# Three, two and two chunks to a batch, groups of experts chosen by sorting, and a new pace table for the GpSimd queue, in a fused sequence-mixer and mixture-of-experts kernel

## What is computed

```python
y = rmsnorm(x); y_conv = conv3(y); y_ssm = scan(h -> tanh(a) * h + b * y)
x = x + y_conv + y_ssm
x1 = layernorm(x_in + x + (silu(z @ w_gate) * (z @ w_up)) @ w_down)      # z = rmsnorm(x)
scores = sigmoid(x1 @ gate_w.T); choice = scores + gate_bias             # 64 experts, 8 groups of 8
group_scores = sum(top_k(choice in groups, 2))                           # best two of each group
mask = groups of top_k(group_scores, 4); top = top_k(where(mask, choice, 0), 8)
w = scores[top] / sum * 2.5
out = layernorm(x1 + sum over top of w * expert(x1) + shared(x1))        # each expert 128 -> 88 -> 128
```

## Time and profile before

| | us |
|---|---|
| median of 3 runs | 884.73 |
| profiled execution | 877.03 |
| its span in the trace | 875.2 |
| TensorE busy | 687.7 (79%) |
| VectorE busy | 481.7 (55%) |
| ScalarE busy | 338.8 (39%) |
| POOL busy (448 indirect DMAs) | 448.5 (51%) |
| chain that ended last: TensorE | 48% |
| same: VectorE | 17% |
| same: "another core or an unknown queue" | 14% |
| same: "issue" | 14% |

### The profile page before, as it was taken

How to read it: one execution, slowest core, us unless ns; L and a number is a source line. 1 busy time by engine, 2 the same in 40 slices (tenths; PEclk the granted TensorE clock), 3 DMA queues, 4 the chain that set the end, 5 groups by cost and what they waited for, 6 DMA issues and landing times.

```text
span 875.2 us, 13683 instructions
## 1 busy us (share of the span) xinstructions
PE 687.7 (79%) x3808; PEld 539.0 (62%) x3809; DVE 481.7 (55%) x1223; ACT 338.8 (39%) x673; POOL 448.5 (51%) x463
## 2 busy tenths in 40 slices
PE   4986777877577689898898889951499899488994
PEld 3654555554344578787788879940488786255662
DVE  3488466872166546555555566710135357275877
ACT  7772544623322134444334444520144443042332
POOL 0002755656656766666676662067466644667300
PEclk9998878998688799999999999985599999799998
DMA  8998931101201246666666666642276646131100
GB/s 272 420 291 341 410 159 40 44 33 45 96 34 40 72 146 188 183 180 186 189 179 184 183 174 189 185 117 64 77 192 184 176 133 205 48 93 45 28 24 24
DMA packets 141798, 128.49 MB, mean 147 GB/s; under 512 B 11542, under 2 KB 127086, under 8 KB 141294
## 3 DMA queue, kind: packets, MB, share of 16 engines
q1 hardware_dynamic: 127430, 98.73, 36.3%
q0 software_dynamic: 14336, 29.39, 10.8%
HBM read 56.77 MB, written 71.30 MB: 146 GB/s over the span
## 4 chain that ended last, share of the span: by engine, by line
PE 48%; DVE 17%; another core or an unknown queue 14%; issue 14%; ACT 5%; DVEq 1%; DMA 0%; ACTq 0%; SPq 0%
PE OT L863 9%; PE GU L843 9%; PE HT L852 4%; PE XT L832 4%; PE GU L900 3%; PE GU L901 3%; PE XT L909 3%; PE OT L645 2%; DVE arena L1483 2%; PE GU L624 2%; PE GU L625 2%; DVE key L1570 1%; ACT x1r L981 1%; PE OT L791 1%
## 5 line engine op out<-in xcount | busy, mean ns | idle before, releaser
L538 POOL DMA_INDIRECT xs_dram<-x1r,slots x224 | 226.9, 1013 | 203.8 <-DVE slots L1357 78.3
L546 POOL DMA_INDIRECT arena<-os_dram,slots x224 | 219.4, 980 | 168.3 <-DMA os_dram<-ol 54.9
L1474 DVE TENSOR_TENSOR mlpw_sb<-GU,mlpw_sb 128x352 f32<-128x352 f32 x104 | 54.5, 524 | 200.5 <-ACT mlpw_sb L1097 111.1
L843 PE MATMUL GU<-wgu_sb,arena 128*128 x832 | 151.6, 327 | 3.5 <-issue 2.9
L863 PE MATMUL OT<-wd_sb,arena 88*128 x832 | 116.2, 283 | 28.5 <-issue 26.4
L843 PEld LDWEIGHTS GU<-wgu_sb,arena 128*128 128x128 f32 x832 | 130.8, 198 | 10.3 <-issue 9.9
L863 PEld LDWEIGHTS OT<-wd_sb,arena 88*128 88x128 f32 x832 | 102.6, 194 | 38.9 <-issue 38.6
L1107 ACT ACTIVATE ol<-OT 128x512 f32<-128x512 f32 x104 | 62.0, 596 | 163.2 <-PE OT L863 97.5
L852 PE MATMUL HT<-ident,mlpw_sb 128*88 128x128 f32 x416 | 63.9, 277 | 33.4 <-DVE arena L1483 31.8
L1090 ACT ACTIVATE arena<-XT 128x512 f32<-128x512 f32 x104 | 61.9, 596 | 46.1 <-remote 26.8
L832 PE MATMUL XT<-ident,arena 128*128 128x128 f32 x416 | 66.7, 284 | 14.1 <-ACT arena L1090 12.8
(11 more groups left out here) (183 smaller groups left out, 913.5 us busy)
## 6 DMA issues: line engine op xcount, KB each, us to landing
arena<-xs_dram SPq DMA_DIRECT2D x104, 256.0 KB
os_dram<-ol SPq DMA_DIRECT2D x104, 256.0 KB
xs_dram<-ol SPq DMA_DIRECT2D x8, 2048.0 KB, 14.6
xs_dram<-ol SPq DMA_DIRECT2D x4, 2560.0 KB
wgu_sb<-wgu_dram SPq DMA_DIRECT2D x1, 5632.0 KB
xs_dram<-x1r,slots POOLq DMA_INDIRECT x224
arena<-os_dram,slots POOLq DMA_INDIRECT x224
wd_sb<-wd_dram SPq DMA_DIRECT2D x1, 2816.0 KB
```

The source lines that it names most:

```text
L538: g.indirect_dma_start(out=xs[b], out_offset=bass.IndirectOffsetOnAxis(ap=slots[:, c:c + 1], axis=0), in_=x1r[:, t, :], in_offset=None).th ...
L546: return g.indirect_dma_start(out=gbuf[:, c % 2, i, k, :], out_offset=None, in_=os[batch_of(c)], in_offset=bass.IndirectOffsetOnAxis(ap=sl ...
L843: ins = mm(GU[:, 2 * r + i // 2, (i % 2) * 2 * I:(i % 2 + 1) * 2 * I], xg[:, r, i * P:(i + 1) * P], wgu_sb[:, bass.ds(at[i], 2 * I)], star ...
```

## The change

Three edits are made together.

Batches: the first batch takes chunks 0, 1 and 2 (40 quads), the second 3 and 4 (32), the third 5 and 6 (32). `EARLY` becomes 2. `Q0` becomes 0, 40, 72, 104. Chunk 1 is summed from quad 68 on instead of 64, and the sums, statistics and one root in the dense stage move by 0 to 2 steps.

Routing: the best two of each group are found by pairwise maxima and minima. The best four groups are found by sorting (`max` gives a row's 8 values in order), the last four of the sorted values are overwritten, and `match_replace` marks the others in the scores.

POOL's table: `POOL_AT`, `FRONT_END`, `SHARED_AT` and `QUADS_AT` get new numbers.

```diff
-BATCHES = (2, 3, 2)
+BATCHES = (3, 2, 2)
...
-SUM_AT = (14, 16, 21, 24)
+SUM_AT = (14, 17, 21, 24)
...
-SUMS_IN_DENSE = {6: 4, 21: 5, 36: 6}
-STATS_IN_DENSE = {0: 0, 1: 1, 2: 2, 3: 3, 14: 4, 29: 5}
+SUMS_IN_DENSE = {8: 4, 22: 5, 36: 6}
+STATS_IN_DENSE = {0: 0, 1: 1, 2: 2, 3: 3, 16: 4, 30: 5}
...
-ROOT_AT = (5, 30)
+ROOT_AT = (5, 31)
...
-POOL_AT = 86.0
+POOL_AT = 100.0
...
-QUADS_AT = 261.0
+QUADS_AT = 256.0
...
+            pairs = flat(group[:, 0:3, :]).rearrange("p (g n) -> p g n", n=3)
...
-                then(v.tensor_reduce(m1, ch4, AX_X, ALU.max))
-                then(v.tensor_tensor(ta4, ch4, bc(m1.unsqueeze(2), P, n, EG), ALU.is_equal))
-                v.tensor_reduce(ties, ta4, AX_X, ALU.add)
-                then(v.scalar_tensor_tensor(out=tb4, in0=ta4, scalar=-BIG, in1=ch4, op0=ALU.mult, op1=ALU.add))
+                lo, hi = ch4[:, :, 0:EG // 2], ch4[:, :, EG // 2:EG]
+                v.tensor_tensor(ta4[:, :, 0:4], lo, hi, ALU.max)
+                then(v.tensor_tensor(ta4[:, :, 4:8], lo, hi, ALU.min))
+                v.tensor_tensor(tb4[:, :, 0:2], ta4[:, :, 0:2], ta4[:, :, 2:4], ALU.max)
+                v.tensor_tensor(tb4[:, :, 2:4], ta4[:, :, 0:2], ta4[:, :, 2:4], ALU.min)
+                then(v.tensor_tensor(tb4[:, :, 4:6], ta4[:, :, 4:6], ta4[:, :, 6:8], ALU.max))
...
-                v.tensor_reduce(m2, tb4, AX_X, ALU.max)
-                then(v.tensor_scalar(ties, ties, 1.5, -BIG, ALU.is_lt, ALU.mult))
-                then(v.tensor_tensor(ties, ties, m1, ALU.add))
-                then(v.tensor_tensor(m2, m2, ties, ALU.max))
-                then(v.tensor_tensor(gs, m1, m2, ALU.add))
+                then(v.tensor_tensor(tb4[:, :, 6:8], tb4[:, :, 2:4], tb4[:, :, 4:6], ALU.max))
+                v.tensor_tensor(pairs[:, :, 0:1], tb4[:, :, 0:1], tb4[:, :, 1:2], ALU.add)
+                then(v.tensor_tensor(pairs[:, :, 1:3], tb4[:, :, 0:2], tb4[:, :, 6:8], ALU.add))
+                then(v.tensor_reduce(gs, pairs, AX_X, ALU.max))
...
-                then(v.tensor_tensor(ta5, other, mine, ALU.is_equal))
-                v.tensor_tensor(tb5, other, mine, ALU.is_gt)
-                then(v.tensor_tensor(ta5, ta5, bc(lower_g[:, :, :].unsqueeze(1), P, CT, NG, NG), ALU.mult))
+                for i in range(CT):
+                    ins = v.max(gtop[:, i, :], gs[:, i * NG:(i + 1) * NG])
+                then(ins)
+                then(v.memset(gtop[:, :, TOPG:NG], NOWHERE))
+                for i in range(CT):
+                    ins = v.match_replace(out=m1[:, i * NG:(i + 1) * NG], in_to_replace=gtop[:, i, :],
+                                          in_values=gs[:, i * NG:(i + 1) * NG], imm_value=GONE)
+                then(ins)
...
-                then(v.tensor_tensor(ta4, ta4, tb4, ALU.add))
-                then(v.tensor_reduce(m1, ta4, AX_X, ALU.add))
-                then(v.tensor_scalar(m2, m1, TOPG - 0.5, None, ALU.is_lt))
+                then(v.tensor_scalar(m2, m1, GONE, None, ALU.is_equal))
```

More of the change, by code:

```diff
@@ L59 @@
 GONE = -3e38
+NOWHERE = -2e38
 FAR = float(1 << 20)
-BATCHES = (2, 3, 2)
+BATCHES = (3, 2, 2)
 NBAT = len(BATCHES)
@@ L92 @@
 EVERY = 1
-POOL_AT = 86.0
-FRONT_END = {2: 76.0, 3: 106.0, 4: 127.0, 5: 146.0, 6: 165.0, 7: 181.0}
-SHARED_AT = 192.0
-QUADS_AT = 261.0
+POOL_AT = 100.0
+FRONT_END = {3: 92.5, 4: 121.0, 5: 140.5, 6: 159.5, 7: 176.5}
+SHARED_AT = 187.5
+QUADS_AT = 256.0
 def progress():
@@ L224, in build @@
         top = sb("top", [P, CT, K])
+        gtop = sb("gtop", [P, CT, NG])
         wsum = sb("wsum", [P, 2, NT])
@@ L1277, in mlp_out @@
                 ins.then_inc(s_mv, 1)
-            m1, m2, ties, gs = (group[:, i, :] for i in range(4))
+            m1, m2, _, gs = (group[:, i, :] for i in range(4))
+            pairs = flat(group[:, 0:3, :]).rearrange("p (g n) -> p g n", n=3)
             by_group = "p t (g e) -> p (t g) e"
@@ L1283, in group_sums @@
             def group_sums(c):
-                n = CT * NG
                 dve.wait_ge(s_sc, c + 1)
                 then(v.tensor_tensor(choice, score, bc(gbias_sb[:, :].unsqueeze(1), P, CT, E), ALU.add))
-                then(v.tensor_reduce(m1, ch4, AX_X, ALU.max))
-                then(v.tensor_tensor(ta4, ch4, bc(m1.unsqueeze(2), P, n, EG), ALU.is_equal))
-                v.tensor_reduce(ties, ta4, AX_X, ALU.add)
-                then(v.scalar_tensor_tensor(out=tb4, in0=ta4, scalar=-BIG, in1=ch4, op0=ALU.mult, op1=ALU.add))
@@ L1294, in group_seconds @@
-            def group_seconds():
-                v.tensor_reduce(m2, tb4, AX_X, ALU.max)
-                then(v.tensor_scalar(ties, ties, 1.5, -BIG, ALU.is_lt, ALU.mult))
-                then(v.tensor_tensor(ties, ties, m1, ALU.add))
-                then(v.tensor_tensor(m2, m2, ties, ALU.max))
-                then(v.tensor_tensor(gs, m1, m2, ALU.add))
-            def compare_groups():
[L1303 to L1306, removed]
-                then(v.tensor_tensor(ta5, other, mine, ALU.is_equal))
-                v.tensor_tensor(tb5, other, mine, ALU.is_gt)
-                then(v.tensor_tensor(ta5, ta5, bc(lower_g[:, :, :].unsqueeze(1), P, CT, NG, NG), ALU.mult))
+                lo, hi = ch4[:, :, 0:EG // 2], ch4[:, :, EG // 2:EG]
```

## The result

The changed kernel takes 834.43 us in the median (831.6 to 838.28, four runs) against 885.33 us for the kernel before on the same chip: a ratio of 0.9461, 95% interval 0.9431 to 0.9491. The forecast was 837. Its profiled execution took 833.4 us, with a span of 831.7. The medians are 50.9 us apart, the two profiled executions 43.6, because the one of the kernel before was a short one of its kind (877.03 against a median of 885.33). What follows divides the 43.5 us between the two spans; the other 7 show in no trace.

The account below looks back on a forecast made before the run. TensorE sets the quads' pace, with holes where late POOL catches up unheld. Terms -30 + 4 - 14 - 4 - 4 = -48 us from the 884.7 us median give 837 us; range 823 to 860 for 8 in 10.

Parts of the forecast that it names:

- What bounds it: Quads and dense stage: TensorE sets the pace; POOL late, then catching up unheld, stretches handoffs between all other engines.
- The price of a held DMA: Quads: each indirect DMA held by the table costs 0.27 us, paid 448 times in either kernel.
- term 1: Quads: the second batch's wait for quad 71's store and the hole after it go, -30 us.
- term 2: First gather: a new wait for quad 39's store makes POOL some 7 us late once, +4 us.
- a hole near quad 40 behind a long wait at the first gather: Quads: set as a sign that the prediction is wrong; no size given for the sign.
- Term 3: Dense stage: the late POOL start at gather 160, with two steps taking 21.1 us, goes: -14 us.
- term 4: Front end: POOL starts one step later, so fifteen fewer scatters come ahead of the quads, -4 us.
- term 5: Front end: the new group selection takes 4.8 us a chunk instead of 6.6, -4 us in all.
- The place theory: Quads: hole belongs to quad 72's loop and batch start, so stays; 876 us, half staying 856; together chance 0.12.
- The slower rival: First gather: POOL's lateness moves there and grows to 71 us, costing 53 us; 890 us, chance 0.05.
- POOL would be the last: Dense stage: POOL's last gathers fall behind and VectorE waits; +8 at worst, 845 us, chance 0.08.
- the 36 that was set as a sign of error: Dense stage: POOL's last gather, due at step 33, coming later than step 36 would show the prediction wrong.

Follow-up runs that it names:

- experiment 6: Changed kernel with the table's waits left out, so POOL is never held: 1186.34 us, ratio 1.3553 to the kernel before.
- experiment 7: Kernel before, its table 40 us later from indirect DMA 288 on, on a disturbing chip: 837.22 us against 882.42, ratio 0.9475.
- experiment 2: Changed kernel, table 7 us later from indirect DMA 224 on, on an undisturbed chip: 702.4 us, ratio 0.9971 to the kernel before.
- 3: Changed kernel, table 7 us earlier for indirect DMAs 224 to 299, on an undisturbed chip: 702.82 us, ratio 0.9981 to the kernel before.
- 10: Changed kernel, table 40 us earlier for indirect DMAs 240 to 300 so POOL runs freely there, on an undisturbed chip: 702.21 us, ratio 0.9978.
- experiment 8: Changed kernel, table 7 us later from indirect DMA 224 on, on a disturbing chip: 836.04 us against 882.42, ratio 0.9465.
- experiment 4: Changed kernel with the old group selection put back, on an undisturbed chip: 706.91 us, ratio 1.0034 to the kernel before.
- experiment 12: Kernel before with the new group selection and table 40 us later from DMA 288 on, old batches, undisturbed chip: 696.84 us, ratio 0.9922.
- experiment 1: Kernel before, its table 40 us later from indirect DMA 288 on, on an undisturbed chip: 704.21 us against 703.72, ratio 1.0001.
- experiment 9: Changed kernel without the table's waits, one memset and wait after each indirect DMA, on a disturbing chip: 1038.56 us, ratio 1.1744.
- 11: Changed kernel without the table's waits, two memsets and waits after each indirect DMA, on an undisturbed chip: 866.68 us, ratio 1.2319.

## Why the prediction was right, point by point

**What bounds it.** Right. POOL late, then running freely, is what makes the hole: experiment 6 makes holes in the front end by freeing POOL, and in the quads and the dense stage as well (34.5 and 51.2 us from one quad's copy to the next at quads 41 and 42), and experiment 7 removes both old holes by moving the table alone. Stated too generally, though: it holds where the result was taken and on two of the four chips of the experiments. On the two others POOL runs at its full rate beside TensorE and nothing stretches. And "the handoffs stretch" isn't all of it: in experiment 6 TensorE's own issue slowed down as well.

**The number.** The 48 us forecast lie between the 50.9 of the medians and the 43.5 of the traces. The terms can be held against the traces alone, and there their sum is 4.5 us too large, so the closeness of 837 to 834.43 says less than it seems.

**The price of a held DMA (0.27 us).** Borne out between chips: the changed kernel takes 829 to 834 us on the first kind, and its close kin (experiments 2, 3 and 10) 702 to 703 on the second, so (831 - 702) / 448 = 0.29 us for each indirect DMA. Up to the first scatter the two kinds run alike: it starts at 101.16 us in the changed kernel and at 101.07 in experiment 2. From there, trace against trace of these two, a DMA costs 0.34 us ahead of the quads (45.0 / 132), 0.30 in them (73.6 / 247) and 0.18 behind them (12.5 / 69).

**Terms 1 and 2, the quads: -26 forecast, -22.4 measured.** With the hole near quad 40 taken as term 2 (+6.7, see below), term 1 is -29.1 where -30 was forecast. Its mechanism is shown by experiment 7, which keeps the long wait and loses the hole. The row of that kernel says more than I had seen: the 41 silent us there aren't lost, since the quads run through them at the undisturbed pace. It wasn't the moved wait that paid, only that the table and the wait now agree. Term 2 was right on the wait (5.59 us for about 7) and on the hole near quad 40, which takes 10.4 - 3.7 = 6.7 us in the trace. The sign of error that the prediction gave for it, a hole near quad 40 behind a long wait at the first gather, so came about in small. What it costs the whole isn't shown: taking it away gained nothing that a ratio shows (experiment 8), which can't tell 4 us from none.

**Term 3, the dense stage: -14 forecast, -10.3 measured.** The late start at gather 160 went and with it the 21 us for two steps. The size was off because I priced the steps under POOL at 2.69 us from the earlier trace rows; 27 steps in 78 us are 2.89, and 35 of them were started before POOL's last gather at 795.4 us, not 33.

**Terms 4 and 5, ahead of the quads: -8 forecast, -10.8 measured.** The first scatter came at 101.16 (98 to 104 forecast) and the first quad at 303.89 (302 to 310). Ahead of the first quad's copy 132 indirect DMAs start where 147 did: the fifteen fewer of term 4. VectorE in order of time, one new selection:

```profile
69.86 0.41 DVE L1290 TENSOR_TENSOR arena<-arena,gbias_sb 128x256 f32<-128x256 f32 x1
...
71.46 0.20 DVE L1299 TENSOR_TENSOR arena<-arena 128x64 f32<-128x64 f32 x1
...
77.16 0.36 DVE L1307 MAX8 gtop<-group 128x8 f32<-128x8 f32 x4
...
78.66 0.17 DVE L1318 TENSOR_SCALAR group<-group 128x32 f32<-128x32 f32 x1
...
79.66 1.23 DVE L1248 TENSOR_TENSOR_SCAN arena<-tanh_a,arena 128x512 f32<-128x512 f32 x1
```

Sums 1.5 us (69.86 to the reciprocal at 71.37), seconds 0.9, comparison 1.2 and mask 1.0: 4.6 us where 4.8 was forecast and 6.6 stood before. The comparison, with 12 instructions on 8 columns, was the unknown: `max` takes 154 ns and `match_replace` 151 at that size, and they overlap so that each pair costs 0.14 us. Experiments 4 and 12 give the selection 4.1 to 5.5 us of the whole, on chips of the second kind; on the first kind it was never separated. That the two terms together come near is partly luck. On those chips the selection alone brings the first quad forward by 12.5 us (experiment 4 against 2) or 8.4 (experiment 12 against 1), where term 5 has 4, and part of this falls in the shared stage, for which it has 0. The new batches and table put it back by 7.2 us (264.18 in experiment 1, 271.38 in experiment 4), where term 5 has 1.2. The rule that I set against it (the Trainium skill, VectorE: DVE Perf Modes, the section on the TRN2 errata: a fixed extra latency for each instruction) agrees with the rows, where 8 columns still take 154 ns, and doesn't decide: the sum is shorter all the same, because ten passes over 256 columns, of 0.42 us each, went in the whole selection: four from the sums and six from the rest ("The change" says five, and leaves out the reduction at L1295).

**The rivals.** The place theory fell with experiment 7, where quad 74 and its loop are unchanged and the hole is gone, and with it the fetch of an instruction page as its cause: a page is fetched in healthy stretches too (one from 577 to 600 us in experiment 7), and none is fetched where experiment 6 has its longest handoffs. The slower rival was right in direction and far too cheap. I priced POOL running ahead of its table at 0.75 us for each us of lateness, 890 us in all; the run that frees it takes 1186. By chips again, (1186 - 703) / 448 = 1.08 us a DMA, nearly the 1.25 us from one to the next: long free runs stop the others almost entirely, where held ones take 0.29. In the earlier trace rows that could be read: in the 53.5 us hole TensorE was busy for a quarter of the time. That POOL would be the last didn't come about; its last gather starts at dense step 35, two later than forecast and one short of the 36 that was set as a sign of error.

**What stays open.** Whether the dose is density or the pause's tie to TensorE (in the dense stage of experiment 9 distance alone was enough; for the quads 9 and 11 don't settle it), whether the effect grows step by step with lateness (3 and 10 met the wrong chip), what in the chip carries it, and why chips differ.

## What to carry to other kernels

A queue that is paced by a table has to be re-timed whenever a data wait is moved past it: a wait that makes the paced engine late was harmless here, and the unheld catching up behind it was what cost. Before moving work to avoid such a wait, try moving the pace alone; it is one number, and here it gave a gain of the same size as three edits together (experiment 7). And price a background DMA from a stretch where it is silent against one where it is held and one where it runs freely: three prices, here 0, 0.29 and about 1.1 us each on the chips that disturb.

## What the runs showed of the hardware

- Of the four chips of the experiments, two disturb (before: 873 and 882 us, and 885 where the result was taken) and two don't (704 and 703 us): 20% between chips for one program, with 3.71 or 3.00 us a quad, and the same 0.94 to 0.97 us for most indirect DMAs on POOL. A gain of 5% on the one kind is 0.2 to 0.3% on the other (experiments 2, 3 and 10, whose tables differ a little from the changed kernel's; the changed kernel itself wasn't run there).
- On the disturbing chips a single handoff between engines took up to 52 us while POOL issued indirect DMAs back to back (`MI` from 130.2 to 182.39 us in experiment 6), without the DMA engines being busy (23% in that stretch). TensorE's own instructions came 1.40 us apart there for 86 us.
- The distance that does harm isn't the same in every stage: 1.4 us from DMA to DMA left the dense stage of experiment 9 alone and broke its quads.
- TensorE's granted clock went to 0.5 to 0.6 of full speed in the holes, its level of 1.2 GHz, when TensorE had had little work: 0.59 in the earlier trace rows, where it was 1.00 in the stretch ahead, and 0.56 in experiment 6. It came back once the work ran on, to 0.74 in the 57 us behind that stretch of experiment 6 and to 1.00 in the changed kernel's stretch from 475 us, behind 0.80.
